# A graph attention kernel: VectorE works on pairs of units in the edge stage

## The reference

```
xn = layernorm(h) ; Q, K, V = xn @ wq + bq, xn @ wk + bk, xn @ wv + bv   # 8 heads of 32
w_phys   = (silu(rbf @ w1 + b1) @ w2 + b2) * cutoff[:, None]
msg_phys = xn[col] * w_phys
scores   = sum(Q[row] * K[col], per head) / sqrt(32) * cutoff
attn     = softmax(scores, over the 8 heads)
msg_attn = attn * V[col]
aggr     = segment_sum(msg_phys + gate * msg_attn, row)
out      = x + h + aggr @ wo + bo
```

## Time and profile before

| what | value |
|---|---|
| median of 3 runs | 5557.56 us (5555.09 to 5559.14) |
| the profiled execution: its time, its span | 5559.19 us, 5557.3 us |
| PE busy | 5156.6 us, 93% |
| DVE busy | 4493.7 us, 81% |
| POOL busy | 4001.3 us, 72% |
| ACT busy | 3260.9 us, 59% |
| edge stage: first query_key to last attend | 2606.1 us to 5436.9 us of the span |

### The profile page before, as it was taken

One profiled execution on the slowest core, in us unless ns is written; L12 is line 12 of the kernel. 1 busy time (PEld: TensorE's weight loads), 2 busy tenths in 40 slices (PEclk: granted clock), 3 DMA queues, 4 the chain that ended last, 5 costly groups with the idle time before them and its releaser, 6 DMA issues. The chain is left out here.

```text
span 5557.3 us, 119878 instructions
## 1 busy us (share of the span) xinstructions
PE 5156.6 (93%) x24352; PEld 3906.9 (70%) x24353; DVE 4493.7 (81%) x11381; ACT 3260.9 (59%) x11609; POOL 4001.3 (72%) x3475
## 2 busy tenths in 40 slices
PE   3879999999999999995899999999999999999999
PEld 3556666666666666674677777777777777777777
DVE  9789887666655555323899999999999999999995
ACT  4223333333333333332788888888888888888884
POOL 1567777777777777775577777777777777777770
PEclk9889999999999999997899999999999999999999
DMA  6234444444444443445999999999999999999965
GB/s 200 89 105 133 144 165 158 142 150 167 158 145 148 168 155 134 152 156 181 314 320 326 325 326 326 325 321 326 325 326 325 326 325 327 324 326 327 326 198 185
DMA packets 584358, 1305.93 MB, mean 235 GB/s; under 512 B 81230, under 2 KB 384118, under 8 KB 582945
## 3 DMA queue, kind: packets, MB, share of 16 engines
q0 software_dynamic: 221536, 881.08, 44.7%
q1 hardware_dynamic: 311780, 345.48, 20.5%
q10 hardware_dynamic: 50850, 77.03, 3.9%
HBM read 1024.15 MB, written 324.38 MB: 243 GB/s over the span
## 5 line engine op out<-in xcount | busy, mean ns | idle before, releaser
L1002 POOL DMA_INDIRECT ukvx<-kvx_table,udst x1760 | 2174.7, 1236 | 668.3 <-issue 480.9
L338 POOL DMA_INDIRECT records<-rows,slot_i x1660 | 1750.9, 1055 | 666.6 <-issue 498.2
L691 PE MATMUL w_ps<-w2s,hid 128*128 128x256 f32 x6656 | 1555.7, 388 | 47.4 <-DVE rows L605 47.3
L691 PEld LDWEIGHTS w_ps<-w2s,hid 128*128 128x128 f32 x6656 | 1251.4, 193 | 371.9 <-issue 156.9
L805 ACT ACTIVATE hid<-hid_ps,b1t 128x512 f32<-128x512 f32 x832 | 525.5, 682 | 1518.5 <-PE hid_ps L680 1504.1
L605 DVE TENSOR_TENSOR rows<-w_ps,b2b 128x512 f32<-128x512 f32 x832 | 570.9, 686 | 749.0 <-PE w_ps L691 748.9
L1118 PE MATMUL ag_ps<-ukvx,uonehot_cut 128*128 128x256 f32 x3520 | 989.3, 404 | 5.3
L1103 PE MATMUL uq_ps<-aggr,uonehotT 128*128 x3520 | 986.4, 404 | 0.0
L1122 PE MATMUL ag_ps<-ukvx,uonehot 128*128 128x256 f32 x3520 | 941.2, 392 | 41.1 <-ACT uonehot L1036 41.1
L1122 PEld LDWEIGHTS ag_ps<-ukvx,uonehot 128*128 128x128 f32 x3520 | 689.0, 196 | 139.7 <-issue 42.2
L1118 PEld LDWEIGHTS ag_ps<-ukvx,uonehot_cut 128*128 128x128 f32 x3520 | 604.8, 192 | 153.9 <-issue 6.3
(11 more groups left out here) (171 smaller groups left out, 5025.0 us busy)
## 6 DMA issues: line engine op xcount, KB each, us to landing
urec<-records SPq DMA_DIRECT2D x880, 260.0 KB
rbf_in<-in_edge_attr SPq DMA_DIRECT2D x207, 256.0 KB, 2.9
kvx_table<-kvx ACTq DMA_DIRECT2D x10, 3456.0 KB, 14.7
ukvx<-kvx_table,udst POOLq DMA_INDIRECT x1760
records<-rows,slot_i POOLq DMA_INDIRECT x1661, 2.6
records<-kvx SPq DMA_DIRECT2D x1, 13000.0 KB
fbase<-x_plus_h SPq DMA_DIRECT2D x14, 896.0 KB, 7.2
out<-fout SPq DMA_DIRECT2D x13, 896.0 KB, 4.9
```

The lines of the kernel that those rows point to most:

```text
L338: pool.indirect_dma_start(recs, bass.IndirectOffsetOnAxis(ap=slot_i[:, q, t:t + 1], axis=0), rows[:, q, t, :], None).then_inc(scattered[q] ...
L691: m = pe.matmul(w_ps[j % 2][:, h, :], hid[:, k % 2, c, h, j * P:(j + 1) * P], w2s[:, c, :], start=(h == 0 and c == 0), stop=(c == 1), skip ...
L1002: pool.indirect_dma_start(kvx[:, k, j, :], None, table, bass.IndirectOffsetOnAxis(ap=dst_i[:, k, j:j + 1], axis=0), bounds_check=NPAD - 1, ...
```

## The change

DVE does all steps except query_key for two units in one operation: at the even unit physical for both units of the pair, and invert and attend for the pair before; at the odd unit score, weigh and maximum for the pair, and then select for the units u+3 and u+4. Each such operation raises its semaphore by 2. The select is now one tensor_tensor of 512 elements instead of four tensor_scalar of 128. ACT's exponent is done at odd units alone, four activations in a row. The score tiles have two places for pairs. The order of ACT is otherwise as it was, and PE, POOL and SP are unchanged.

```diff
-        sc = sb("uscores", [P, 2, 2, NH])
+        sc = sb("uscores", [P, 2, 4, NH])
...
             def exponent(u, k, i, first):
-                q = k % 2
+                q = k // 2 % 2
                 act.wait_ge(s["max_done"], u + 1)
-                if not (first and k < 2):
-                    act.wait_ge(s["av_done"], u - 1)
-                for j in range(2):
-                    m = act.activation(ex[:, q, j, :], sc[:, q, j, :], ACT.Exp, bias=mx[:, q, j:j + 1], accum_out=sm[:, q, j:j + 1])
-                m.then_inc(s["exp_ready"], 1)
+                if not (first and k < 4):
+                    act.wait_ge(s["av_done"], u - 3)
+                for r in range(4):
+                    m = act.activation(ex[:, q, r, :], sc[:, q, r, :], ACT.Exp, bias=mx[:, q, r:r + 1], accum_out=sm[:, q, r:r + 1])
+                m.then_inc(s["exp_ready"], 2)
...
                 ahead(cut_off, OUT_AHEAD, u, k, i, first, last)
                 ahead(destinations, GATHER_AHEAD, u, k, i, first, last)
                 behind(share, 2, u, k, i, first)
-                exponent(u, k, i, first)
+                if k % 2:
+                    exponent(u, k, i, first)
...
             def select(u, k, i, first):
-                dve.wait_ge(rec_in[k], i * 16 + 16)
+                for n in range(2):
+                    dve.wait_ge(rec_in[k + n], i * 16 + 16)
                 if not first:
-                    dve.wait_ge(s["cut_ready"], u - (DEPTH - 1))
-                    dve.wait_ge(s["share_ready"], u - (DEPTH - 1))
-                    dve.wait_ge(s["turned"], u - (DEPTH - 1))
-                for j in range(2):
-                    m = dve.tensor_scalar(ohb[:, k, j, :], iota_bf[:], rec[:, k, j, R_LOC:R_LOC + 1], None, ALU.is_equal)
-                m.then_inc(s["onehot_ready"], 1)
+                    dve.wait_ge(s["cut_ready"], u - (DEPTH - 2))
+                    dve.wait_ge(s["share_ready"], u - (DEPTH - 2))
+                    dve.wait_ge(s["turned"], u - (DEPTH - 2))
+                dve.tensor_tensor(pair(ohb, k), iota_bf[:].unsqueeze(1).to_broadcast([P, 4, P]),
+                                  pair(rec, k)[:, :, R_LOC:R_LOC + 1].to_broadcast([P, 4, P]), ALU.is_equal).then_inc(s["onehot_ready"], 2)
...
             def physical(u, k, i, first):
-                dve.tensor_tensor(kvx[:, k, :, 2 * H:3 * H], rec[:, k, :, 0:H], kvx[:, k, :, 2 * H:3 * H], ALU.mult).then_inc(s["phys_done"], 1)
+                dve.wait_ge(kvx_in[k + 1], i * 32 + 32)
+                both = pair(kvx, k)[:, :, 2 * H:3 * H]
+                dve.tensor_tensor(both, pair(rec, k)[:, :, 0:H], both, ALU.mult).then_inc(s["phys_done"], 2)
...
             def unit(u, k, i, first, last):
                 query_key(u, k, i, first)
-                physical(u, k, i, first)
-                ahead(select, SELECT_AHEAD, u, k, i, first, last)
-                score(u, k, i, first)
-                behind(invert, 1, u, k, i, first)
-                weigh(u, k, i, first)
-                maximum(u, k, i, first)
-                behind(attend, 1, u, k, i, first)
+                if k % 2 == 0:
+                    physical(u, k, i, first)
+                    behind(invert, 1, u, k, i, first)
+                    behind(attend, 1, u, k, i, first)
+                else:
+                    score(u, k, i, first)
+                    weigh(u, k, i, first)
+                    maximum(u, k, i, first)
+                    ahead(select, SELECT_AHEAD - 1, u, k, i, first, last)
```

More of the change, by code:

```diff
@@ L915, in edges @@
         ohT = sb("uonehotT", [P, 4, 2, P])
-        sc = sb("uscores", [P, 2, 2, NH])
[L917 to L920, removed]
+        sc = sb("uscores", [P, 2, 4, NH])
+        mx = sb("umax", [P, 2, 4])
+        ex = sb("uexp", [P, 2, 4, NH])
+        sm = sb("usum", [P, 2, 4])
+        rc = sb("urecip", [P, 2, 4])
         turn_ps = ps("turn_ps", [P, 8, P], BF16)
@@ L1035, in share @@
                 for j in range(2):
[L1036 removed]
+                    m = act.activation(oh[:, k, j, :], ohb[:, k, j, :], ACT.Copy, scale=rc[:, k // 2 % 2, k % 2 * 2 + j:k % 2 * 2 + j + 1])
                 m.then_inc(s["share_ready"], 1)
             def exponent(u, k, i, first):
[L1040 removed]
+                q = k // 2 % 2
                 act.wait_ge(s["max_done"], u + 1)
[L1042 to L1046 removed]
+                if not (first and k < 4):
[3 more added lines that the diff above has]
+                m.then_inc(s["exp_ready"], 2)
             def keep(u, b):
@@ L1163, in _, with pair @@
         def _(dve):
+            def pair(tile, k):
+                return tile[:, k:k + 2].rearrange("p k j e -> p (k j) e")
             def select(u, k, i, first):
-                dve.wait_ge(rec_in[k], i * 16 + 16)
+                for n in range(2):
+                    dve.wait_ge(rec_in[k + n], i * 16 + 16)
                 if not first:
-                    dve.wait_ge(s["cut_ready"], u - (DEPTH - 1))
-                    dve.wait_ge(s["share_ready"], u - (DEPTH - 1))
-                    dve.wait_ge(s["turned"], u - (DEPTH - 1))
-                for j in range(2):
-                    m = dve.tensor_scalar(ohb[:, k, j, :], iota_bf[:], rec[:, k, j, R_LOC:R_LOC + 1], None, ALU.is_equal)
-                m.then_inc(s["onehot_ready"], 1)
+                    dve.wait_ge(s["cut_ready"], u - (DEPTH - 2))
[3 more added lines that the diff above has]
+                                  pair(rec, k)[:, :, R_LOC:R_LOC + 1].to_broadcast([P, 4, P]), ALU.is_equal).then_inc(s["onehot_ready"], 2)
             def query_key(u, k, i, first):
@@ L1186, in score @@
                 dve.wait_ge(s["qk_done"], u + 1)
-                if not (first and k < 2):
-                    dve.wait_ge(s["exp_ready"], u - 1)
-                dve.tensor_reduce(sc[:, q], kvx[:, k, :, 0:H].rearrange("p j (h d) -> p j h d", h=NH), AX_X, ALU.add).then_inc(s["scored"], 1)
+                if not (first and k < 4):
+                    dve.wait_ge(s["exp_ready"], u - 3)
+                dve.tensor_reduce(sc[:, q], pair(kvx, k - 1)[:, :, 0:H].rearrange("p r (h d) -> p r h d", h=NH), AX_X, ALU.add).then_inc(s["scored"], 2)
@@ L1191, in weigh @@
             def weigh(u, k, i, first):
-                q = k % 2
+                q = k // 2 % 2
                 dve.wait_ge(s["scored"], u + 1)
-                dve.scalar_tensor_tensor(sc[:, q], sc[:, q], float(HD) ** -0.5, rec[:, k, :, R_CUT:R_CUT + 1].to_broadcast([P, 2, NH]), ALU.mult, ALU.mult).then_inc(s["weighted"], 1)
+                dve.scalar_tensor_tensor(sc[:, q], sc[:, q], float(HD) ** -0.5, pair(rec, k - 1)[:, :, R_CUT:R_CUT + 1].to_broadcast([P, 4, NH]), ALU.mult, ALU.mult).then_inc(s["weighted"], 2)
@@ L1196, in maximum @@
             def maximum(u, k, i, first):
-                q = k % 2
+                q = k // 2 % 2
                 dve.wait_ge(s["weighted"], u + 1)
-                dve.tensor_reduce(mx[:, q], sc[:, q], AX_X, ALU.max, negate=True).then_inc(s["max_done"], 1)
+                dve.tensor_reduce(mx[:, q], sc[:, q], AX_X, ALU.max, negate=True).then_inc(s["max_done"], 2)
             def invert(u, k, i, first):
-                q = k % 2
+                q = k // 2 % 2
                 dve.wait_ge(s["exp_ready"], u + 1)
-                if not (first and k < 2):
-                    dve.wait_ge(s["share_ready"], u - 1)
@@ L1206, in invert @@
-                dve.reciprocal(rc[:, q], sm[:, q]).then_inc(s["recip_done"], 1)
+                if not (first and k < 4):
+                    dve.wait_ge(s["share_ready"], u - 3)
+                dve.reciprocal(rc[:, q], sm[:, q]).then_inc(s["recip_done"], 2)
             def attend(u, k, i, first):
-                q = k % 2
+                q = k // 2 % 2
                 dve.wait_ge(s["exp_ready"], u + 1)
-                dve.tensor_tensor(kvx[:, k, :, H:2 * H].rearrange("p j (h d) -> p j h d", h=NH),
-                                  kvx[:, k, :, H:2 * H].rearrange("p j (h d) -> p j h d", h=NH),
-                                  ex[:, q].unsqueeze(3).to_broadcast([P, 2, NH, HD]), ALU.mult).then_inc(s["av_done"], 1)
+                values = pair(kvx, k - 1)[:, :, H:2 * H].rearrange("p r (h d) -> p r h d", h=NH)
@@ L1215, in _ @@
+                dve.tensor_tensor(values, values, ex[:, q].unsqueeze(3).to_broadcast([P, 4, NH, HD]), ALU.mult).then_inc(s["av_done"], 2)
             dve.tensor_copy(ident_bf[:], ident[:]).then_inc(s["narrow"], 1)
@@ L1219, in _ @@
             dve.wait_ge(s["narrow"], 2)
-            for k in range(SELECT_AHEAD):
+            for k in range(0, SELECT_AHEAD, 2):
                 select(k, k, 0, True)
```

2 lines of the change are left out of this document (1 added, 1 removed).

## The result

The changed kernel takes 5900.6 us (median of 4 runs, 5896.4 to 5906.2) against 5557.4 us beside it: 1.062 of the kernel before, 95% interval 1.060 to 1.064.

The account below looks back on a forecast made before the run. DVE was taken to set the pace, PE close behind. Four ring pairs of 7.42 us plus 0.33 (k = 0) and 0.88 (clock) gave 30.9 us a turn against 25.32: +607 us over 109 turns, 6165 us, range 6030 to 6320.

Parts of the forecast that it names:

- The place of select decides: DVE's late select holds evacuate(u+3), which ACT does before exponent(u), so the pair's exponents start late; a pair takes 7.42 us.
- its ring: Select, PE transpose, ACT evacuate and exponents, DVE invert to the next select: 7.42 us a pair, DVE idle about 1.4.
- DVE waits before L1206 for ACT's exponents: Sign in the profile after: this wait once a pair, about 1.4 us, 440 times, some 600 us.
- DVE's busy share: Sign in the profile after: DVE's busy share in the edge stage falls to about 76%.
- ACT's waits for the transposes: Sign in the profile after: ACT waits before L1023 for PE's transpose at odd units; no size given.
- 5.74 us fit into a pair: PE's work for two units, 2 x 2.87 = 5.74 us, fits into the pair's 7.42 us.
- k = 0: Where PE and ACT read registers: PE reaches its next transpose at about S + 7.81 (S: select's end), 0.33 us more a turn.
- register reads take longer when they begin at S: Rival at k = 0: reads begun at select's end, without a lead, cost another 1 us a turn; 6275 us, chance 0.08.
- The clock: PE's half-clock stretch after the k = 0 pause costs 1.75 us more in half of the turns: 0.88 a turn.
- DVE's own work: DVE's steps for a pair, without waits for other engines, take 5.87 us against 6.33 before.
- the rival that gave 5505 us: Rival: ring does not close, DVE's saving shows, PE bounds with 24.8 us a turn; -55 us, chance 0.05.
- Records and rows in time: SP's records and the gathered rows still arrive in time in the paired kernel; costed at nothing.

Follow-up runs that it names:

- out_three: Changed kernel with ACT evacuating and cutting off three units ahead instead of two: 6939.5 us, 1.125 of the kernel before.
- select_even: Changed kernel with the paired select moved to the even unit behind physical, for units u+4 and u+5: 0.988 of the kernel before, again 0.989.
- before_late: Kernel before, nothing paired, its select moved from behind physical to the end of the unit, for u+3: 1.019 of the kernel before, again 1.010.
- no_reads: Changed kernel without PE's register reads in the loop, all edges summed into bucket 0: 0.971 of the kernel before.
- warm: Changed kernel with three filling matmuls on constants queued on PE before the register reads of k = 0: 0.993 of the kernel before.
- before_warm: Kernel before with three filling matmuls ahead of PE's register reads and nothing else: 0.983 of the kernel before.
- before_again: Kernel before, unchanged, run for a profile on the chip of its neighbours: 0.999 of the kernel before.

## Why the prediction was wrong

- **The step that failed is "The place of select decides": that exponent(u) stands behind an evacuate which needs the select of the same unit.** It stands behind evacuate(u+2), whose select is a pair older. out_three, with the number that the prediction assumed, shows its ring with 8.05 us a pair and the idle time before invert; the changed kernel shows neither. That DVE waits before L1206 for ACT's exponents, the first thing that was to show it, is refuted by 1.5 us in 140 inverts. DVE's busy share is 83% and not 76%, a turn 28.6 us and not 30 to 31. ACT's waits for the transposes (142 times in 140 pairs) and the select of 0.70 us did come as written, but they fit either ring.
- **What stands in its place** is a ring with the length of a turn, not of a pair: 28.04 us in the turn shown, against 25.32 before. It runs through the step that the prediction had rightly named as moved: the select for u+3 as the last of the odd unit, and PE's turn(u+3) in the same unit. The price was seen only for ACT. For PE I wrote that 5.74 us fit into a pair. They do, but the register reads of k = 0 had been started ahead of DVE, and now start behind the select. select_even takes the late select out and before_late puts it in alone, and the loss goes and comes; no_reads takes the reads out, and DVE's wait for PE goes. These runs show the links on chips with a loss of 1.2 to 1.4%; that the same ring makes up the 6.2% of the first chip rests on its trace, whose ring adds up to the measured turn.
- **k = 0.** The prediction has L1115 2.90 us behind the transpose; it is 3.94 (4007.60 to 4011.54), and 3.95 as the median. The rival "register reads take longer when they begin at S" named this, with "another 1 us a turn", and was right; it was priced on top of a ring that did not exist. The reads were never just 1.87 us long: without them the gap is 1.04 us (no_reads), so they cost 2.9 us where nothing hides them, and before the change part of that had been hidden.
- **The clock.** Named, with 0.88 us a turn more. By the clock's mean it is 1.5 us more of PE's time, and 1.89 us in the turn shown. warm shows it on the path; before_warm shows that on the other chips it is on the path of the kernel before as well.
- **DVE's own work.** 5.87 us a pair were forecast and 6.36 measured. Products of 1024 elements are as worked out (medians 1.14 and 1.11 for 1.13). The dependences are not: 0.77 for 0.71, 1.33 for 1.24, 0.30 for 0.23, and maximum to select 0.30 for 0.11. In the kernel before other operations stood ahead of score and of weigh, and the order by pairs took them away; maximum stood right behind weigh there too, but 0.04 us after its end, where it is now 0.11. So the rival that gave 5505 us had no saving to show. The new select takes 697 ns for 512 elements, the 0.68 that the products gave and the Trainium skill's rule ("VectorE: DVE Perf Modes", section "What auto-detection actually checks") spoke for.
- **Records and rows in time: costed at nothing.** Not quite: DVE waits 14.4 us in 1000 for gathered rows at L1188, and ACT 29.9 us for records, 0.4 and 0.9 us a turn. No run here separates them; they are part of what lies between the 28.04 us of the turn shown and the mean of 28.57.
- The direction came out right, with a mechanism that was wrong in the engine and in the length of its ring. That the two losses, 343 and 607 us, are of one order is chance.

## What to carry to other kernels

Before a step is moved in a hand-written order, list each consumer of it with the number of units that it runs ahead, copied from the line that sets it, and check on the timeline that one pair of rows has this distance: one look at which unit's evacuate stands before exponent would have refuted the ring. A wait that is harmless seven times out of eight can cost at the eighth, where something long (register reads) had been hidden by the lead that the wait takes away. And one operation for two units saves little beyond a start-up (1.14 and 1.11 us for 2 x 0.60 in the products here); where it also brings dependent operations next to each other, part of that is given back, 0.06 to 0.09 us at each such place beyond what I had reckoned.

## What the runs showed of the hardware

- The same two kernels have a ratio of 1.062 on one chip and of 1.014 and 1.012 on two others, on which both are slower. There ACT, DVE and POOL show waits that the profile puts down to "remote", which neither trace of the first chip has. In 1000 us of before_again:

```profile
ACT uonehotT L1023 <- remote: 85.7, 68, 2.8
...
DVE ukvx L1179 <- remote: 55.7, 24, 2.7
```

What they are stays open. PE's lead is shorter there in the kernel before too (a read gap of 3.51 us for 2.83), which fits with the late select losing less; that these waits are the reason is not shown.
- On the other two chips, a PE pause of up to 2.6 us once in 28 us costs about 2% of the whole time through the clock behind it, in the kernel before as in the changed one, and three matmuls on constants, queued ahead of the register reads, hold the clock at 0.99 to 1.00 (0.92 to 0.94 without).
- Reading 27 values into PE's registers costs 2.9 us between a transpose and the next matmul when nothing hides it (3.95 us, against 1.04 without the reads).
- A short DVE operation that depends on the one before starts about 0.11 us after its end (weigh 4021.65 + 0.19 to maximum 4021.95), not 0.04 as in the earlier trace rows; the select behind maximum, which depends on nothing of it, starts 0.12 to 0.21 us after its end. I had expected such gaps to be the same whatever stands before; why they differ was not tried.
